# Swin-style megakernel on one core: fifth head's Q and K computed with the values, a new order of each strip step, and the last 32 channels transposed together

## The reference, cut to what matters

```python
x = _ln(x, ln1g, ln1b)
xw = _win_part(x)
qkv = xw @ qkvw + qkvb
q, k, v = jnp.split(qkv, 3, axis=-1)
...
attn = softmax(einsum('whid,whjd->whij', q, k) * HEAD_DIM ** (-0.5) + bias + mask)
out = jnp.einsum('whij,whjd->whid', attn, v)
out = out @ projw + projb
x = sc + _win_rev(out, Bb)
h = _ln(x, ln2g, ln2b)
return x + jax.nn.gelu(h @ w1 + b1) @ w2 + b2
```

## Time and profile before

| | us |
|---|---|
| median of three runs | 2950.62 |
| the profiled execution: its own time | 2952.52 |
| its span, first to last instruction | 2951.0 |
| TensorE busy in the span | 2883.9 (98%) |
| DVE (VectorE) busy | 2213.6 (75%) |
| ACT (ScalarE) busy | 1721.5 (58%) |
| GpSimd (POOL) busy | 837.1 (28%) |
| mean granted TensorE clock | 0.986 of full speed |

### The profile page before, as it was taken

How to read it: one execution, slowest core, us unless ns; L and a number is a source line. 1 busy time by engine, 2 the same in 40 slices (tenths; PEclk the granted TensorE clock), 3 DMA queues, 4 the chain that set the end, 5 groups by cost and what they waited for, 6 DMA issues and landing times. The chain is left out here.

```text
span 2951.0 us, 94022 instructions
## 1 busy us (share of the span) xinstructions
PE 2883.9 (98%) x39898; PEld 2703.9 (92%) x39898; DVE 2213.6 (75%) x6736; ACT 1721.5 (58%) x4076; POOL 837.1 (28%) x1470
## 2 busy tenths in 40 slices
PE   8979999999999999999999999999999999999799
PEld 6669999999999999999999999999999999999799
DVE  5667777887787777787788878778878878887422
ACT  6446666666666666666656655565656555665321
POOL 8122222222222222222323322232323332332111
PEclk9969999999999999999999999999999999999899
DMA  6321111111111111111112221121111111112374
GB/s 155 128 90 25 40 46 43 46 43 46 43 43 30 42 43 46 43 46 43 46 26 47 58 58 34 33 44 44 42 24 44 44 44 25 42 43 46 65 136 77
DMA packets 210768, 152.23 MB, mean 52 GB/s; under 512 B 15954, under 2 KB 205205, under 8 KB 210331
## 3 DMA queue, kind: packets, MB, share of 16 engines
q1 hardware_dynamic: 207619, 142.41, 21.0%
q10 hardware_dynamic: 1008, 3.44, 0.5%
q0 software_dynamic: 1728, 0.48, 0.2%
HBM read 95.64 MB, written 52.50 MB: 50 GB/s over the span
## 5 line engine op out<-in xcount | busy, mean ns | idle before, releaser
L1627 PE MATMUL rm<-w,ht 128*112 128x160 f32 x4480 | 676.5, 300 | 0.0
L1627 PEld LDWEIGHTS rm<-w,ht 128*112 128x112 f32 x4480 | 619.7, 177 | 11.8
L1051 POOL TENSOR_TENSOR rs<-ln_tmp,mhalf 112x4 f32<-112x4 f32 (+1 forms) x128 | 118.8, 928 | 980.3 <-DVE ln_tmp L1233 980.3
L1148 ACT ACTIVATE ht<-rm 128x336 f32<-128x336 f32 (+1 forms) x448 | 216.6, 490 | 124.6 <-PE rm L147 124.5
L1091 ACT ACTIVATE qm<-ra,qpair 128x400 f32<-128x400 f32 x256 | 138.1, 590 | 214.4 <-PE ra L147 214.4
L1124 ACT ACTIVATE pt<-pt_ps 113x490 f32<-113x490 f32 x256 | 149.4, 584 | 184.7 <-PE pt_ps L1566 184.7
L1005 POOL TENSOR_TENSOR z<-z,one 112x448 f32<-112x448 f32 (+2 forms) x192 | 131.4, 684 | 358.2 <-DVE z L1237 358.2
L1119 ACT ACTIVATE pr<-sm 113x490 f32<-113x490 f32 x256 | 159.5, 623 | 88.4 <-DVE sm L1296 87.7
L1338 DVE TENSOR_TENSOR ot_lo<-ra,ot_hi 128x98 fp32r<-128x98 f32 x512 | 109.1, 255 | 128.1 <-ACT ot_rest L1131 118.0
L1131 ACT ACTIVATE ot_hi<-ra 128x98 fp32r<-128x98 f32 x512 | 102.1, 259 | 141.3 <-PE ra L1601 141.3
L1296 DVE TENSOR_TENSOR sm<-sc,mx 113x490 f32<-113x490 f32 x256 | 177.6, 694 | 6.6
(11 more groups left out here) (276 smaller groups left out, 9231.8 us busy)
## 6 DMA issues: line engine op xcount, KB each, us to landing
xa<-xs SPq DMA_DIRECT2D x128, 245.0 KB
xr<-xs SPq DMA_DIRECT2D x128, 245.0 KB
xs<-xo SPq DMA_DIRECT2D x64, 245.0 KB
ys<-yz SPq DMA_DIRECT2D x64, 245.0 KB
c_y<-ys SPq DMA_DIRECT2D x36, 260.0 KB
xs<-a_tok SPq DMA_DIRECT2D x14, 560.0 KB, 6.1
xs<-tok_late SPq DMA_DIRECT2D x14, 560.0 KB, 6.7
a_nat<-in_x ACTq DMA_DIRECT2D x7, 480.0 KB, 6.2
```

Of the source, the lines that this page charges most:

```text
L1148: act_(ht[:, f * SN + t0 * TT:f * SN + (t0 + nt) * TT], bank_m(i, lm, use)[:, 0:nt * TT], ACT.Gelu_apprx_tanh).then_inc(m_freed(i, lm, use ...
L1627: last = mm(bank_m(i, lm, use)[0:TT, t * DIM:(t + 1) * DIM], ht[:, c:c + TT], keep.w["w2", lm][:, f * DIM:(f + 1) * DIM], start=(f == 0), ...
```

## The change

1. **Fifth head.** The product B goes. `values` now multiplies by columns 256 to 480 of the weights, that is the fifth head's Q (32) and K (32) and the 160 value columns: 224 moving columns instead of 160. ACT's `values` copies the value columns into `vb` and the fifth head's columns, tokens by channels, into the new tile `qk5`. TensorE's new `fifth_head` turns these with 8 small float32 matmuls against the identity per half strip (49 x 64 stationary, 49 moving), and ACT's `fifth_head` copies the result out in three instructions of 196 columns (one 128 partitions high, two 32).
2. **Turns.** z has 160 columns per tile again; GpSimd's `rest_apart` gathers the last 32 channels of all tiles of a half strip side by side in `z1r` or `z2r`. One transpose per half strip then turns four (or three) tiles' rest together, into 128 (or 96) rows, 32 per tile. ACT's high copies and DVE's subtractions of the C part are done per tile: 4 or 3 instructions of 32 x 112 in place of one of 448 or 336 columns. The third copy of the rest rows is a further ACT copy from SBUF to SBUF (`front_rest`, `t_rest`). The first product's last pass waits for the rest rows by itself (`rest_ready`).
3. **Order.** All four engines get new lists, and the bank orders with them. `xa_normalised` of the next strip moves to the same step that turns it, between `t_lo(1)` and `outputs_lo(0)`; `xa_stats` moves behind `mlp_out(0)`.

TensorE's new order is: T2 of half 0, outputs(0), scores(2), weights_turned(1), G0 to G2, T2 of half 1, G3, G4, OT0, outputs(1), scores(3), G5 to G9, (layer 1: linear), T1A0, T1C0, T1A1, the first token tile of W0, T1C1, OT1, the rest of W0, weights_turned(2), V0, V1, Q, K and the fifth head of half 0, W1, outputs(2), scores(0) of the next strip, weights_turned(3), W2, OT2, outputs(3), scores(1), W3, OT3, weights_turned(0), V2, the first two matmuls of W4, the projections, Q of half 1, V3, the rest of W4, W5, the fifth head and K of half 1.

ACT's new order, from the last gelu on: front_hi A0, C0, A1, front_rest(0), exps(2), front_hi C1, front_rest(1), outputs_hi(1), weights_out(2), exps(3), values(0), values(1), queries(0), keys(0), fifth_head(0), weights_out(3), outputs_hi(2), exps(0), outputs_hi(3), weights_out(0), values(2), exps(1), queries(1), values(3), fifth_head(1), keys(1). Ahead of it `t_rest(0)` stands behind `t_hi(0)` and `t_rest(1)` behind `t_hi(1)`. On DVE, besides the hunk below, `mlp_out(2)` goes between scores_max(0) and scores_less_max(0), outputs(3) ahead of outputs_lo(2), outputs_lo(3) ahead of scores_max(1), and `mlp_out(4)` behind residual(2). GpSimd copies z1's rest ahead of `inv_std` of the strip after next.

The diff, cut to its core (t_hi and t_lo are changed as front_hi and front_lo are):

```diff
+        if n == 3:
+            for ready in rest_ready:
+                nc.tensor.wait_ge(*ready)
...
-        RA = Ring(["T1A0", "T1C0", "OT1", "T1A1", "T1C1", "Q0", "K0", "B0", "V0", "V1", "OT2", "OT3", "P0", "P1", "P2",
-                   "Q1", "B1", "K1", "V2", "V3", "T2A1", "T2C1", "OT0"], 3, {})
+        RA = Ring(["T1A0", "T1C0", "T1A1", "T1C1", "OT1", "V0", "V1", "Q0", "K0", "B0", "OT2", "OT3", "V2", "P0", "P1", "P2",
+                   "Q1", "V3", "B1", "K1", "T2A1", "T2C1", "OT0"], 3, {})
...
-        T2_USES = [("T2A0", 0), ("T2C0", 1)]
-        G_USES = [(f"G{g}", n) for g, n in enumerate((2, 1, 0, 2, 1, 0, 1, 2, 0, 1))]
-        L_USES = [("L0", 2), ("L1", 0), ("L2", 1), ("L3", 2)]
-        W_USES = [(f"W{n}", n % 2) for n in range(len(PAIRS))]
+        T2_USES = [("T2A0", 1), ("T2C0", 0)]
+        G_USES = [(f"G{g}", n) for g, n in enumerate((1, 0, 2, 1, 0, 2, 1, 0, 2, 1))]
+        L_USES = [("L0", 0), ("L1", 2), ("L2", 1), ("L3", 0)]
+        W_USES = [(f"W{n}", (n + 1) % 2) for n in range(len(PAIRS))]
...
+            def rest_apart(t, r, s, t0=0, nt=ST):
+                gp.tensor_tensor(view(r, 0, TT, t0 * REST, [[REST, nt], [1, REST]]),
+                                 view(t, 0, TT, t0 * DIM + 128, [[DIM, nt], [1, REST]]),
+                                 view(one, 0, TT, 0, [[0, nt], [0, REST]]), ALU.mult).then_inc(s, 1)
...
+                def front_hi(part, hf):
                     t0, nt = HALF[hf]
-                    for part, dst, rows in (("A", z1t[0], 128), ("C", z1t[2], CR)):
-                        use = f"T1{part}{hf}"
-                        act.wait_ge(*a_full(i, use))
-                        act_(view(dst, 0, rows, t0 * WIN, [[WIN, nt], [WP, 16], [1, WIN]]),
-                             view(bank_a(i, use), 0, rows, 0, [[TT, nt], [WIN, 16], [1, WIN]]), ACT.Copy).then_inc(s_hi1, 1)
+                    use = f"T1{part}{hf}"
+                    act.wait_ge(*a_full(i, use))
+                    if part == "A":
+                        last = act_(view(z1t[0], 0, 128, t0 * WIN, [[WIN, nt], [WP, 16], [1, WIN]]),
+                                    view(bank_a(i, use), 0, 128, 0, [[TT, nt], [WIN, 16], [1, WIN]]), ACT.Copy)
+                    else:
+                        for t in range(nt):
+                            last = act_(view(z1t[2], 0, REST, (t0 + t) * WIN, [[WP, 16], [1, WIN]]),
+                                        view(bank_a(i, use), t * REST, REST, 0, [[WIN, 16], [1, WIN]]), ACT.Copy)
+                    last.then_inc(s_hi1, 1)
+
+                def front_rest(hf):
+                    t0, nt = HALF[hf]
+                    dims = [[WP, 16], [1, nt * WIN]]
+                    act.wait_ge(s_hi1, (i + 1) * 4 + 2 * hf + 2)
+                    act_(view(z1t[2], 2 * REST, REST, t0 * WIN, dims), view(z1t[2], 0, REST, t0 * WIN, dims).bitcast(F32),
+                         ACT.Copy).then_inc(s_rest1, 1)
...
+                    act_(q4[:, cols], bank_a(i, use)[:, 0:2 * GK], ACT.Copy, scale=float(HD) ** -0.5)
                     for p in range(2):
-                        act_(view(q4, p * WP, HD, hf * QH + p * WQ, dims), view(bank_a(i, use), 0, HD, p * WQ, dims), ACT.Copy,
-                             scale=float(HD) ** -0.5)
-                        last = act_(view(k4, p * WP, HD, hf * QH + p * WQ, dims), view(bank_a(i, use), HD, HD, p * WQ, dims),
-                                    ACT.Copy)
+                        last = act_(k4[p * WP:p * WP + HD, cols], bank_a(i, use)[p * WP + HD:(p + 1) * WP, 0:2 * GK], ACT.Copy)
                     last.then_inc(a_freed(i, use)[0], 1)
...
+                    act_(view(vb, 0, QP, j * VJ, [[HEADS * VW, 2], [VW, HEADS], [1, HD]]),
+                         view(bank_a(i, use), 0, QP, 2 * HD, [[VC, 2], [HD, HEADS], [1, HD]]), ACT.Copy)
+                    act_(view(qk5, 0, QP, j % 2 * 128, [[2 * HD, 2], [1, 2 * HD]]),
+                         view(bank_a(i, use), 0, QP, 0, [[VC, 2], [1, 2 * HD]]), ACT.Copy).then_inc(a_freed(i, use)[0], 1)
...
+                    dims = [[WP, 16], [1, WIN]]
+                    dve.wait_ge(s_hi1, (i + 1) * 4 + 2 * hf + 2)
+                    for t in range(nt):
+                        ins = v.tensor_tensor(view(z1t[2], REST, REST, (t0 + t) * WIN, dims),
+                                              view(bank_a(i, f"T1C{hf}"), t * REST, REST, 0, [[WIN, 16], [1, WIN]]),
+                                              view(z1t[2], 0, REST, (t0 + t) * WIN, dims).bitcast(F32), ALU.subtract)
+                    ins.then_inc(a_freed(i, f"T1C{hf}")[0], 1)
...
+                if la is not None and ln is not None:
+                    xa_normalised(i + 1)
                 if la is not None:
                     outputs_lo(0)
-                if la is not None:
                     scores_biased(3, i, la)
                     scores_max(3, i)
                     scores_less_max(3, i)
@@ -1414,43 +1457,39 @@
                 if lm == 1:
                     for n in range(len(LPAIRS)):
                         linear_out(n)
-                if more and la is not None:
-                    xa_stats(i + 2)
                 if ln is not None:
                     front_lo(0)
+                    front_lo(1)
                 if la is not None:
                     outputs_lo(1)
-                if ln is not None:
-                    front_lo(1)
-                if la is None and lm is None:
-                    xa_stats(1)
                 if lm is not None:
                     mlp_out(0)
                 if more:
-                    xa_normalised(i + 2)
+                    xa_stats(i + 2)
...
+            def turn(z, zr, hf, bank_of, room, full, name, freed_already=(), parts="AC"):
                 t0, nt = HALF[hf]
-                for part, f0, rows in (("A", 0, 128), ("C", 128, CR)):
+                for part in parts:
                     use = f"{name}{part}{hf}"
                     if use not in freed_already:
                         reach(pe, *room(use))
-                    for t in range(nt):
-                        c = (t0 + t) * ZW + f0
-                        last = tr(bank_of(use)[0:rows, t * TT:(t + 1) * TT], z[:, c:c + rows], keep.ident[0:TT, 0:TT])
+                    if part == "A":
+                        for t in range(nt):
+                            c = (t0 + t) * DIM
+                            last = tr(bank_of(use)[:, t * TT:(t + 1) * TT], z[:, c:c + 128], keep.ident[0:TT, 0:TT])
+                    else:
+                        last = tr(bank_of(use)[0:nt * REST, 0:TT], zr[:, t0 * REST:(t0 + nt) * REST],
+                                  keep.ident[0:TT, 0:TT])
                     last.then_inc(full(use), 1)
...
+                    wv = [w[:, 2 * 128:3 * DIM] for w in keep.w["qkv", ln]]
                     for w in range(2):
                         c = slice((8 * w + 2 * j) * WP, (8 * w + 2 * j) * WP + QP + 1)
-                        last = split_passes(nc, bank_a(n, use)[0:QP + 1, w * DIM:(w + 1) * DIM], *[t[:, c] for t in z1t], *wv, False)
-                    last.then_inc(a_full(n, use)[0], 1)
+                        last = split_passes(nc, bank_a(i, use)[0:QP + 1, w * VC:(w + 1) * VC], *[t[:, c] for t in z1t], *wv, False,
+                                            rest_ready=[(s_rest1, 2 * (i + 2)), a_freed(i, "T1C1")] if j == 0 and w == 0 else ())
+                    filled_a(use, last)
...
+                def fifth_head(hf):
+                    use = f"B{hf}"
+                    pe.wait_ge(*a_freed(i, f"V{2 * hf + 1}"))
+                    if hf == 1:
+                        room_a(use)
+                    for n in range(4):
+                        for p in range(2):
+                            rows = slice(p * WP, p * WP + WT)
+                            last = mm(bank_a(i, use)[p * WP:(p + 1) * WP, n * WT:(n + 1) * WT], qk5[rows, n * WP:(n + 1) * WP],
+                                      keep.ident[rows, rows], start=True, stop=True)
+                    filled_a(use, last)
...
+                    front_turned(1, "A")
+                if lm is not None:
+                    mlp_out(0, 0, FT)
+                if ln is not None:
+                    front_turned(1, "C")
                 if la is not None:
                     outputs_turned(1)
                 if lm is not None:
-                    mlp_out(0)
-                if ln is not None:
-                    front_turned(1)
+                    mlp_out(0, FT)
```

More of the change, by code:

```diff
@@ L1182, in body @@
                 if ln is not None:
+                    values(0)
+                    values(1)
                     queries(0)
@@ L1451, in body @@
                     scores_less_max(1, i + 1)
-                if lm is not None:
-                    mlp_out(4)
                 if la is not None:
@@ L1462, in body @@
                     residual(2)
+                if lm is not None:
+                    mlp_out(4)
+                if la is not None:
```

(29 more changed lines are left out.)

184 lines of the change are left out of this document (97 added, 87 removed).

## The result

The changed kernel takes **3105.47 us** (median of four runs, 3104.86 to 3106.23); the kernel before, run beside it, 2950.02. The ratio is 1.0522, 95% interval 1.0504 to 1.0541: 5.2% slower. The forecast was 2997 with a range of 2890 to 3040, so the direction was right and the loss, 155 us, is over three times the +47 that I worked out.

The account below looks back on a forecast made before the run. TensorE's queue bounded the kernel; the change would make it wait on DVE's front: 32 layer 0 steps at +0.34 us and 30 layer 1 steps at +1.2 give +47 on 2950.6, 2997 us, range 2890 to 3040.

Parts of the forecast that it names:

- The pieces held.: ACT's and DVE's 32x112 C-part copies do not overlap: 0.275 us each, 1.10 for four, 0.82 for three.
- where TensorE waits: Waits forecast ahead of OT1 and T1C1, in layer 1 also the last linear block and V0's fourth pass.
- DVE's walk to OT1: Layer 0, front of the step: DVE's instructions summed from T2 to front_lo(0), freeing OT1's bank at 16.05 us.
- From OT1 to the next T2 ... 23.3: Rest of the step on TensorE: 25.28 us before, 23.3 after summing the edit's savings and additions.
- TensorE alone -1.35: TensorE's work per step: fewer transposes, no B passes, wider value passes and new fifth-head matmuls, net -1.35 us.
- It turns into a gain once the front is 0.75 us per step shorter: Front of the step: shortening it by 0.75 us per step on average would turn the loss into a gain.
- ACT's further new work ... I cost at nothing: TensorE's wait on DVE covers it: ACT's qk5 and rest copies, some 4 us per step, costed at nothing; up to 0.3 if DVE were quicker.
- A (pieces overlap): Rival: small pieces on DVE and ACT overlap, 1.4 us off the front, 1.8 in layer 1; 2901 us; 18%.
- my two cases: The forecast with small pieces held, 2997 us, and the rival with them overlapping, 2901 us.
- B: Rival: TensorE stays the bound and no bank is late, -1.35 us per step, 2868 us; 8%.
- C: Rival: pieces held, but the walk is too long by 0.5 to 1 us per step, 2930 to 2965; 14%.
- D: Rival: fifth head runs one tile at a time, +0.7 us per step, 3040 us; 6%.

Follow-up runs that it names:

- e8: The changed kernel with the normalise moved behind mlp_out(0) and all small pieces reading partitions 0 to 31 of the turned bank: 2966.4 us, ratio 1.0057.
- e7: The changed kernel with the normalise moved behind mlp_out(0) and, on ACT, T1C1's pieces and rest copy ahead of exps(2): 3092.3 us, ratio 1.0481.
- e5: The changed kernel with the last channels turned strip by strip and evicted wide as before, and the normalise moved behind mlp_out(0): 2944.5 us, ratio 0.9977.
- e12: e5 with only the second half of the MLP's input (T2C1) turned jointly: 2930.4 us, ratio 0.9934 to the kernel before.
- e3: The changed kernel without GpSimd's addition of the second MLP bias in layer 1 (base_second): 3074.5 us, single run.
- e1: The changed kernel with xa_stats behind front_lo(0) and the normalise behind mlp_out(0), out of DVE's front: 3060.6 us, ratio 1.0375.
- e2: The changed kernel with every small piece reading partitions 0 to 31 of the turned bank, so the input's group never changes: 2996.7 us, single run.
- e4: The changed kernel with the last channels turned strip by strip and evicted wide as before, normalise left early: 2973.0 us, ratio 1.0074.

## Why the prediction was wrong in size and right in direction

**Right: "The pieces held."** 0.275 per piece was taken, 0.269 and 0.259 came; four pieces took 1.12 and three 0.83 on DVE (1.10 and 0.82 forecast). The rule of the Trainium skill ("VectorE: DVE Perf Modes", section "Two Vector instructions with no wait between them") that an instruction is held when one of its operands starts in another quadrant than the last one did agrees with the trace on DVE: 0.269 with the input's group changing, 0.205 without (e8). On ACT the 93 ns of overlap that the Trainium skill states ("ScalarE: Activation LUTs", section "What ACT_TABLE_LOAD costs") shows only where the group stays: 0.250 - 0.172 = 0.08 in e8, and 0.00 in the changed kernel.

**Right: where TensorE waits.** OT1, T1C1, the last linear block and V0's fourth pass, in that order of places.

**Wrong by 0.46 per step: DVE's walk to OT1** (16.05 against 16.51). 0.32 of it is one subtraction, sm at 1035.61, that took 0.99 instead of the 0.67 I had from before. GpSimd ran its additions beside it in both kernels. The addition that was running when the subtraction began had 0.46 left here and 0.13 before. That this made the difference is likely by what the normalise shows, but no run tests it.

**Wrong by 1.0 per step, and the step that failed: "From OT1 to the next T2 ... 23.3".** It took 40.81 - 16.51 = 24.3, and as much too long in layer 1 (44.95 - 19.95 = 25.0 in the median, against 24.0). That is 62 of the 108 us. By distances from start to start in layer 0:
- mlp_out: I let its first tile go (-1.36) and the wait ahead of OT3 (-0.31). The six segments that are left shrank by 1.19 only (9.67 to 8.48), 0.48 less than that.
- Value products: what stands of them behind OT1 grew by 1.24 (2.50 to 3.74), not by 0.88. Of the 0.36, 0.23 is V0's fourth pass waiting for T1C1's pieces in layer 0 too: V0 and V1 take 1.99 here and 1.76 in e7, where that wait is gone. I had seen that ACT comes to T1C1 only after exps(2), but had priced it for layer 1 alone.
- The fifth head's 8 small matmuls (16 records) take 0.60 from start to start, not 0.49: 0.22 for both halves.

The first and the third are no cost of waiting: they are in e5 and e12 as well, whose lists show no wait in those places. "TensorE alone -1.35" therefore was too good: with ten transposes (0.96) back, e5 should have been 38.62 and is 38.89. I had summed only what the edit adds and removes, and had taken every hand-over between segments as unchanged.

**Wrong by 1.0 ahead of OT1 in layer 1** (18.95 against 19.97). The normalise was costed at 2.0 from a mean of 355 ns, measured where GpSimd was quiet. At its new place it takes 2.9; e3 brings the 0.9 back with nothing moved, and e1 by moving it away. I had asked what the moved step delays, and not what runs beside it where it goes.

**The verdict on the cause.** "It turns into a gain once the front is 0.75 us per step shorter" is false: e1 took 2.0 out of DVE's front in layer 0 and gained nothing. I had walked DVE alone, and had written that TensorE's wait on DVE covers ACT's new work, at most 0.3 if DVE were quicker. The runs put about 0.9 there (V0 and V1 2.63 in e1, 1.76 in e7). So "ACT's further new work ... I cost at nothing: TensorE's wait on DVE covers it" is the second step that failed: ACT's chain to V0's fourth pass ends no earlier than DVE's, and behind a quicker DVE it alone keeps the loss.

**Rivals.** A (pieces overlap) was put at 2901; with overlap made to happen, the whole change is 2997 (e2): the saving of 109 is near the 96 between my two cases, from a worse start. Its sum was loose: 11 x 0.095 + 4 x 0.13 is 1.57, of which it used 1.4. B is out. C and D were both out of reach: the fifth head cost 0.11 more each, not 0.35.

## What to carry to other kernels

Fewer instructions on the bounding engine were worth nothing here, since each eviction behind them became four or three in series on two other engines. Ask for each place how long the bounding engine is busy between the turn and the first use of its result, and convert only the places where that is longer than the chain (here T2C1, which gave 14 us; T1's two were tried only together). When an engine's chain seems to set the time, walk the neighbour's chain too before pricing a fix: two that end together hide each other. A moved instruction must be priced with the neighbours of its new place, not of its old one.

## What the runs showed of the hardware that I had not expected

- A DVE TENSOR_SCALAR of 112x160 on SBUF that began 0.05 us behind a GpSimd addition from and to SBUF lasted until 0.10 us past the addition's end, 1.27 us instead of 0.36; its six neighbours were as fast as ever. A mean over the group hides this: 355 to 360 ns where GpSimd is quiet, 418 (after), 434 (e2) and 446 (e4) where one of layer 1's seven is so held.
- ACT's instructions overlap by 0.08 us if the input stays in one group of PSUM partitions, and not at all if it changes: busy 0.172 against 0.259 us per copy of 250 to 259 ns. The change of the input's group alone is enough; the output stays in partitions 0 to 31.
- Sixteen records of transposing float32 matmuls of 49 columns on two tiles take 0.60 us, 38 ns each, three and a half times the 11 ns that each of the score records on four tiles was given in the forecast (0.58 us for 40, less 0.14 of hand-over).
